# Attention inside an adaLN block: score tiles in two groups, and mask and maximum as one VectorE instruction per head and tile

## The chip, the core and the metric

The program runs on one core of one Trainium2 chip. The core has TensorE (PE: matmuls into PSUM, with the weight loads in a row of their own, PEld), VectorE (DVE), ScalarE (ACT), GpSimd (POOL) and SyncE (SP, which only issues DMAs here). The engines run in parallel, each in its own order, and wait for each other by semaphores. The metric is the device time in microseconds (us), the median of several runs.

## The reference, cut to what matters

```
h = layernorm(x) * (1 + ca) + sa                 # x: 8 batches, 512 tokens, 128 features, float32
q, k, v = split(h @ W_qkv)                       # 16 heads of 64
q, k = rotary(q), rotary(k)
s = (q @ k.T) / 8;  s = where(causal, s, -1e9)   # 512 x 512 per head
o = softmax(s) @ v
x = x + ga * (o @ W_out)
h = layernorm(x) * (1 + cb) + sb
x = x + gb * moe(h)                              # 8 experts, the best 2 per token
```

The change touches the attention alone, above all the two lines of the scores: the causal mask and the softmax.

## The kernel before, in words

Attention is done by pairs of heads: 8 batches with 8 pairs each, 64 pairs in all. A loop over slots (`all_slots`, L1419) writes the code of every engine. In a slot three pairs are in work at three stages: `q0` gets its q and k projections and the rotary turn, `q1`, one pair behind, its scores, and `q2`, two behind, the rest of its softmax, the product with v and the output product. Each engine has one function that writes its part of a slot (`pe_slot` L1125, `act_slot` L1218, `dve_slot` L1317, `pool_slot` L1371, `sp_slot` L1401). The order of lines there is the order in the engine's queue: nothing is scheduled later, and an engine that waits holds all that stands behind it.

The scores of a pair come in four tiles of 128 queries. Only the keys up to the diagonal are computed, so the tiles `TILES = (3, 0, 2, 1)` are 512, 128, 384 and 256 keys wide, each for two heads. I call them S512, S128, S384 and S256. A tile and head is a "unit" (0 to 7): units 0 and 1 are S512, 2 and 3 S128, 4 and 5 S384, 6 and 7 S256. One unit takes one PSUM bank. S512 and S384 share banks 2 and 3, S128 and S256 share banks 4 and 5, so S384 can start only when units 0 and 1 have been read by the exponential.

After the scores (`pe_scores`, on 64 rows of the PE array per head) VectorE adds the mask to the diagonal block of both heads (`dve_mask`, L1276) and takes the negated maximum over both (`dve_max`, L1283). ACT computes exp(s - max) with its row sum (`act_exp`, L1171). PE transposes the result block by block (`pe_turn_prob`, L1090) in six turns "3a", "3b", "0", "2a", "2b", "1" of 4, 4, 2, 3, 3 and 4 blocks, which alternate between the PSUM banks 6 and 7. ACT or DVE stores each turn to SBUF (`act_store` L1192, `dve_store` L1298), which frees its bank for the turn after the next. DVE inverts the row sums (L1290), ACT spreads them (`act_rep`, L1215), PE transposes them (`pe_turn_sum`, L1099) and ACT copies them to `rs` (L1209). Then come the product with v (`pe_values`, L1112), its scaling (`dve_ot`, L1306), the output product (`pe_out`, L1121) and its addition to x (`dve_acc`, L1314).

Two banks hold projections. Bank W1 holds k, is read by `dve_u` and `dve_t` (L1262, L1267), and later in the slot holds the output product until `dve_acc` has read it: `pe_qk` (L1027 to L1034) waits for `v_acc`, the `dve_acc` of the slot before. Bank W0 holds q, then the product with v, then the next tile of v (`pe_v`, L1048), which ACT copies (L1203) and whose copy the q half of `pe_qk` waits for. The route functions (`route_pe` and others) put the normalisation and expert routing of other batches into some slots.

Of the kernel before, what the change touches and what calls it, by code (L numbers as in the profile page):

```python
# [12 lines left out]
P = 128  # L13
# [32 lines left out]
MASKED = -1e30  # L46

# [40 lines left out]
def adaln_kernel(nc, x_in, w_qkv, w_out, gate_w, expert_bias, w_up, w_down, c_t, w_mod,  # L88
                 cos_in, sin_in, ident_in, tri_in, rank_in, const_in, out, xs, ys, parts, gates):
    ctx = ExitStack()  # L90
    with ctx:
# [689 lines left out]
        tri = sb(att, "tri", [P, P])  # L781
# [187 lines left out]
        with ExitStack() as ph:  # L969
# [14 lines left out]
             v_u, v_t, v_tk, v_tri, v_max, v_ev, v_rden, v_ot, g_qk, g_lo, g_wo, d_ur) = (  # L984
                sem("b_" + n) for n in (
                    "pqk", "pv", "ps", "pt", "pr", "pvp", "pout", "aexp", "aev", "ahi", "av", "ar", "arep",
                    "vu", "vt", "vtk", "vtri", "vmax", "vev", "vrden", "vot", "gqk", "glo", "gwo",
# [86 lines left out]
            def pe_turn_prob(e, q, u):  # L1074
                n, at = q.n, TURNS.index(u)
                e.wait_ge(a_exp, NU * n + READ[u][-1] + 1)
                if u == "3a":
                    if due(2 * n):
                        e.wait_ge(v_ev, 2 * n)
                elif u == "3b":  # L1080
                    if due(4 * n):
                        e.wait_ge(a_ev, 4 * n)
                elif u == "2a":
                    e.wait_ge(v_ev, 2 * n + 1)
                else:
                    e.wait_ge(a_ev, 4 * n + {"0": 1, "2b": 2, "1": 3}[u])
# [8 lines left out]
            def pe_turn_sum(e, q):  # L1095
                e.wait_ge(a_rep, q.n + 1)
                e.wait_ge(v_tk, min(q.n + 3, STEPS))
                for i in range(TB):
                    mm = e.transpose(ps[:, W1, i * P:(i + 1) * P],  # L1099
# [3 lines left out]
            def pe_values(e, q):  # L1103
# [4 lines left out]
                e.wait_ge(v_t, min(n + 3, STEPS))  # L1108
                v, first = val[q.group], (q.hp % GP) * P
# [15 lines left out]
            def pe_slot(e, i, c):  # L1125
# [7 lines left out]
                if q1.live:  # L1133
                    pe_scores(e, q1, 0)
                if q2.live:
# [3 lines left out]
                if q1.live:  # L1139
                    pe_scores(e, q1, 1)  # L1140
                if q2.live:
                    pe_values(e, q2)
                if q1.live:
                    pe_turn_prob(e, q1, "3a")
                    pe_scores(e, q1, 2)
                if q2.live:
                    pe_out(e, q2)
                if q1.live:
                    pe_turn_prob(e, q1, "3b")
                if v.live:  # L1150
                    pe_v(e, v)
                if c in SPARE:
                    if q1.live:
                        e.wait_ge(a_ev, 4 * q1.n + 1)
                    elif q2.live:
                        e.wait_ge(v_ev, 2 * q2.n + 2)
                    route_pe(e, i, c)
                if q1.live:
                    pe_scores(e, q1, 3)

            def act_exp(e, q, unit):
# [3 lines left out]
                e.wait_ge(v_max, TB * n + idx + 1)  # L1165
# [3 lines left out]
                if unit == 0 and due(n - 1):  # L1169
                    e.wait_ge(v_rden, n - 1)  # L1170
                e.activation(prob[:, unit, 0:w], ps[:, bank_s(idx) + j, 0:w], ACT.Exp,  # L1171
                             bias=nmax[:, q.par, idx, j:j + 1],
# [13 lines left out]
            def act_store(e, q, u):  # L1186
                n = q.n
                e.wait_ge(p_t, 6 * n + TURNS.index(u) + 1)
                if u == "3a" and due(n - 1):
                    e.wait_ge(p_vp, n - 1)  # L1190
# [14 lines left out]
            def act_r(e, q):  # L1205
# [3 lines left out]
                e.copy(rs[:], ps[:, W1, :]).then_inc(a_r, 1)  # L1209
# [8 lines left out]
            def act_slot(e, i, c):  # L1218
# [3 lines left out]
                if q2.live:  # L1222
                    act_exp(e, q2, 5)
                    act_exp(e, q2, 6)
                    act_exp(e, q2, 7)
                    act_store(e, q2, "0")
                    act_store(e, q2, "2a")
                    act_rep(e, q2)
# [5 lines left out]
                if q1.live:  # L1234
# [4 lines left out]
                    act_store(e, q1, "3a")  # L1239
                route_act_part(e, i, c, 1)  # L1240
                if (i, c) == (0, 2):

                    act_v(e, v)
                if q0.live:
                    act_hi(e, q0, 1)
                    act_hi(e, q0, 0)
# [5 lines left out]
                if q1.live:  # L1252
                    act_exp(e, q1, 4)
# [16 lines left out]
            def dve_mask(e, q, idx):  # L1270
                w = (TILES[idx] + 1) * P
                bank = bank_s(idx)
                at = TB * q.n + idx + 1
                e.wait_ge(p_s, at)
                block_ = ps[:, bank:bank + 2, w - P:w]
                e.tensor_tensor(block_, block_, tri[:].unsqueeze(1).to_broadcast([P, 2, P]),  # L1276
                                op=ALU.add).then_inc(v_tri, 1)

            def dve_max(e, q, idx):
                w = (TILES[idx] + 1) * P  # L1280
                bank = bank_s(idx)
                e.wait_ge(v_tri, TB * q.n + idx + 1)
                e.tensor_reduce(nmax[:, q.par, idx, :], ps[:, bank:bank + 2, 0:w], AX.X, ALU.max,  # L1283
# [763 lines left out]
```

## Time and profile before

| | |
|---|---|
| runs | 994.35, 997.01 and 1002.05 us; median 997.01 |
| profiled execution | span 996.9 us (the page gives no other time for it) |
| PE | 907.6 us busy, 91% |
| PE weight loads | 659.0 us, 66% |
| DVE | 830.6 us, 83% |
| ACT | 740.4 us, 74% |
| POOL | 570.1 us, 57% |

The attention fills the span from about 20 to 800 us. The rest is the expert part and the end, which the change leaves alone. Busy time of matmuls is from start to a modelled end, and neighbours overlap, so the starts of matmuls say more than their durations.

### The profile page before, as it was taken

The page shows a single profiled execution, that of the slowest core. Times are in us where ns is not written, and L with a number is a line of the kernel's source. Part 1 is how long each engine was busy: PE and PEld are TensorE (multiplying, and loading weights), DVE is VectorE, ACT ScalarE, POOL GpSimd, SP SyncE. Part 2 cuts the span into 40 slices and gives each one's busy share as a digit, 9 for nine tenths or more (in the row PEclk, how much of TensorE's full clock was granted, in tenths as well). Part 3 has the DMA queues.
Part 4 walks back from the last instruction along what each step waited for, and adds up shares of the span by engine and source line. Part 5 has one row for each costly group of instructions (what it writes and reads, how often), then busy time and mean ns, then how long its engine had stood idle before and what let it go on. Part 6 is the DMA issues. An engine that isn't in the chain of part 4 may idle for free. (4 is left out here: it accounts for less than half of the span.)

```text
span 996.9 us, 21240 instructions
## 1 busy us (share of the span) xinstructions
PE 907.6 (91%) x6278; PEld 659.0 (66%) x6278; DVE 830.6 (83%) x1816; ACT 740.4 (74%) x2070; POOL 570.1 (57%) x687
## 2 busy tenths in 40 slices
PE   5699999999999999999999999999999778999930
PEld 3466667676676677666766767677667556888820
DVE  6588888788988888888888888888998678899847
ACT  4487788878787887788778877787777654777725
POOL 1445456545666477657755675767466356765532
PEclk9799999999999999999999999999999989999975
DMA  8234443333344434433344434333443347899844
GB/s 250 81 93 105 111 109 95 94 93 104 94 109 113 117 99 124 115 93 94 108 118 107 110 112 118 96 100 111 110 108 96 110 162 274 290 317 321 311 136 131
DMA packets 124575, 135.53 MB, mean 136 GB/s; under 512 B 13837, under 2 KB 108571, under 8 KB 120496
## 3 DMA queue, kind: packets, MB, share of 16 engines
q1 hardware_dynamic: 118768, 122.42, 42.5%
q0 software_dynamic: 4544, 8.93, 2.7%
q10 hardware_dynamic: 1152, 2.85, 0.8%
q8 instruction: 52, 0.85, 0.3%
q14 instruction: 59, 0.48, 0.2%
HBM read 51.53 MB, written 39.49 MB: 91 GB/s over the span
## 5 line engine op out<-in xcount | busy, mean ns | idle before, releaser
L1364 POOL TENSOR_TENSOR four<-four 128x512 f32<-128x512 f32 x128 | 161.1, 1280 | 278.7 <-DVE ot L1306 178.2
L1171 ACT ACTIVATE prob<-ps,nmax 128x512 f32<-128x512 f32 (+3 forms) x512 | 264.4, 531 | 51.6 <-DVE nmax L1283 50.9
L1283 DVE TENSOR_REDUCE nmax<-ps 128x2 f32<-128x1024 f32 (+3 forms) x256 | 211.0, 824 | 8.8
L1090 PE MATMUL ps<-ident,prob 128*128 128x128 f32 x1280 | 192.4, 280 | 9.3 <-ACT probt L1192 4.9
L1090 PEld LDWEIGHTS ps<-ident,prob 128*128 128x128 f32 x1280 | 142.3, 141 | 60.3 <-ACT prob L1171 32.8
L1368 POOL TENSOR_TENSOR qk_lo<-four,qk_hi 128x512 fp32r<-128x512 f32 x128 | 163.4, 1300 | 1.5 <-ACT qk_hi L1199 1.5
L1276 DVE TENSOR_TENSOR ps<-ps,tri 128x256 f32<-128x256 f32 x256 | 109.4, 427 | 53.8 <-PE ps L1069 53.3
L1112 PE MATMUL ps<-probt,val 128*64 128x512 f32 (+3 forms) x1024 | 152.6, 440 | 0.0
L1192 ACT COPY probt<-ps 128x512 f32<-128x512 f32 (+2 forms) x256 | 125.2, 524 | 21.1 <-PE ps L1090 21.1
L1199 ACT CAST qk_hi<-four 128x512 fp32r<-128x512 f32 x128 | 79.4, 622 | 79.0 <-POOL four L1364 78.3
L1112 PEld LDWEIGHTS ps<-probt,val 128*64 128x64 f32 x1024 | 68.0, 137 | 74.0 <-issue 59.9
L1064 PE MATMUL ps<-qk_hi 64*128 64x512 f32 (+3 forms) x256 | 105.6, 412 | 5.2 <-POOL qk_lo L1368 5.2
L1990 POOL DMA_INDIRECT results<-y,to_i x78 | 82.3, 1055 | 47.4 <-DVE y L1821 28.8
L1262 DVE TENSOR_TENSOR four<-ps,turn_s 128x1024 f32<-128x1024 f32 x64 | 78.4, 1225 | 35.4 <-PE ps L1034 30.9
L1171 ACT ACTIVATION_READ_ACCUMULATOR prob<-ps,nmax 128x1 f32 x512 | 106.1, 207 | 0.0
L1065 PE MATMUL ps<-qk_hi 64*128 64x512 f32 (+3 forms) x256 | 105.6, 413 | 0.0
L1911 ACT ACTIVATE hf<-ps 128x256 f32<-128x256 f32 (+1 forms) x120 | 53.9, 449 | 39.5 <-PE ps L1762 39.0
L1064 PEld LDWEIGHTS ps<-qk_hi 64*128 64x128 f32 x256 | 47.2, 185 | 53.9 <-issue 33.6
L1067 PE MATMUL ps<-qk_hi,qk_lo 64*128 64x512 f32 (+3 forms) x256 | 82.1, 321 | 0.0
L1066 PE MATMUL ps<-qk_hi,qk_lo 64*128 64x512 f32 (+3 forms) x256 | 82.0, 320 | 0.0
L1069 PE MATMUL ps<-qk_lo,qk_hi 64*128 64x512 f32 (+3 forms) x256 | 82.0, 320 | 0.0
L1068 PE MATMUL ps<-qk_lo,qk_hi 64*128 64x512 f32 (+3 forms) x256 | 82.0, 320 | 0.0
(276 smaller groups left out, 2241.5 us busy)
## 6 DMA issues: line engine op xcount, KB each, us to landing
four<-four SPq DMA_DIRECT2D x252, 128.0 KB
wt<-parts SPq DMA_DIRECT2D x24, 1024.0 KB, 7.2
slots<-fill SPq DMA_DIRECT2D x64, 288.0 KB, 2.8
parts<-split SPq DMA_DIRECT2D x64, 128.0 KB, 2.3
wq_lo<-parts SPq DMA_DIRECT2D x6, 1024.0 KB, 6.3
hb<-h_hi SPq DMA_DIRECT2D x64, 64.0 KB, 2.3
hb<-h_lo SPq DMA_DIRECT2D x64, 64.0 KB, 2.0
plain<-results SPq DMA_DIRECT2D x8, 512.0 KB, 7.5
```

Of the source, the lines that this page charges most:

```text
L1064: e.matmul(o0, hi[top_, 0, cols], hi[top_, 1, 0:w], start=True, stop=False)
L1065: e.matmul(o1, hi[low_, 0, cols], hi[low_, 1, 0:w], start=True, stop=False)
L1067: e.matmul(o1, lo[low_, 0, cols], hi[low_, 1, 0:w], start=False, stop=False)
L1090: mm = e.transpose(ps[:, PT + at % 2, at_block * P:(at_block + 1) * P], prob[:, unit, kk * P:(kk + 1) * P], ident[:])
L1112: mm = e.matmul(ps[j * HD:(j + 1) * HD, W0, kk * P:S], v[:, kk, first + j * HD:first + (j + 1) * HD], probt[q.par][:, j, kk, kk * P:S], st ...
L1171: e.activation(prob[:, unit, 0:w], ps[:, bank_s(idx) + j, 0:w], ACT.Exp, bias=nmax[:, q.par, idx, j:j + 1], accum_out=den[:, q.par, 2 * i ...
L1192: e.copy(dst, src).then_inc(a_ev, 1)
L1276: e.tensor_tensor(block_, block_, tri[:].unsqueeze(1).to_broadcast([P, 2, P]), op=ALU.add).then_inc(v_tri, 1)
L1283: e.tensor_reduce(nmax[:, q.par, idx, :], ps[:, bank:bank + 2, 0:w], AX.X, ALU.max, negate=True).then_inc(v_max, 1)
L1364: e.tensor_tensor(qk[:, cols], tt[:, cols], ur[:, cols], op=ALU.add).then_inc(g_qk, 1)
L1368: e.tensor_tensor(qk_lo[q.par][:, half, :], qk[:, half * S:(half + 1) * S], qk_hi[q.par][:, half, :], op=ALU.subtract).then_inc(g_lo, 1)
L1990: e.indirect_dma_start(ys, bass.IndirectOffsetOnAxis(to_i[:, j % Y, t:t + 1], 0), y4[:, j % Y, t, :], None, bounds_check=2 * B * S - 1, oo ...
```

## The change

On PE the slot is written in another order. Before: projections, turns "0" and "2a", S512, turns "2b" and "1", the sum, S128, values, turn "3a", S384, output, turn "3b", v, routing, S256. Now: projections, turns "0", "2a", "2b", "1", the sum, S512, S128, values, S384, S256, turns "3a" and "3b", output, v, routing. The transposed sum goes to bank 6 in place of W1. The turns "3a" and "3b" are both stored by DVE, and "0", "2a", "2b", "1" all by ACT ("3a" was ACT's, "2b" DVE's).

On DVE the mask and the maximum of a unit are one `tensor_tensor_reduce`: it adds a mask as wide as the tile (`tri` now has 512 columns, all zero but the last 128), multiplies by -1, writes the result to the scores' bank and reduces it by minimum. ACT's exponential now takes scale -1 and waits for one unit in place of a tile of two. All eight maxima of a pair are taken in the slot of its scores; before, S256's were left to the next slot, and so were the exponentials 5 to 7 on ACT.

```diff
+HIGHEST = 3e38
...
-        tri = sb(att, "tri", [P, P])
+        tri = sb(att, "tri", [P, S])
...
                 if u == "3a":
-                    if due(2 * n):
-                        e.wait_ge(v_ev, 2 * n)
+                    if due(4 * n - 1):
+                        e.wait_ge(a_ev, 4 * n - 1)
+                    if due(n):
+                        e.wait_ge(a_r, n)
                 elif u == "3b":
                     if due(4 * n):
                         e.wait_ge(a_ev, 4 * n)
-                elif u == "2a":
-                    e.wait_ge(v_ev, 2 * n + 1)
+                elif u in ("0", "2a"):
+                    e.wait_ge(v_ev, 2 * n + {"0": 1, "2a": 2}[u])
                 else:
-                    e.wait_ge(a_ev, 4 * n + {"0": 1, "2b": 2, "1": 3}[u])
+                    e.wait_ge(a_ev, 4 * n + {"2b": 1, "1": 2}[u])
...
             def pe_turn_sum(e, q):
                 e.wait_ge(a_rep, q.n + 1)
-                e.wait_ge(v_tk, min(q.n + 3, STEPS))
+                e.wait_ge(a_ev, 4 * q.n + 3)
                 for i in range(TB):
-                    mm = e.transpose(ps[:, W1, i * P:(i + 1) * P],
+                    mm = e.transpose(ps[:, PT, i * P:(i + 1) * P],
                                      rrep[:, i, :, :].rearrange("p j f -> p (j f)"), ident[:])
...
+                e.wait_ge(v_tk, min(n + 3, STEPS))
...
@@ -1130,46 +1134,42 @@
                     spare_read(e, i, c - 1)
                     pe_turn_prob(e, q2, "0")
                     pe_turn_prob(e, q2, "2a")
-                if q1.live:
-                    pe_scores(e, q1, 0)
-                if q2.live:
                     pe_turn_prob(e, q2, "2b")
                     pe_turn_prob(e, q2, "1")
                     pe_turn_sum(e, q2)
                 if q1.live:
+                    pe_scores(e, q1, 0)
                     pe_scores(e, q1, 1)
                 if q2.live:
                     pe_values(e, q2)
                 if q1.live:
+                    pe_scores(e, q1, 2)
+                    pe_scores(e, q1, 3)
                     pe_turn_prob(e, q1, "3a")
-                    pe_scores(e, q1, 2)
+                    pe_turn_prob(e, q1, "3b")
                 if q2.live:
                     pe_out(e, q2)
-                if q1.live:
-                    pe_turn_prob(e, q1, "3b")
                 if v.live:
                     pe_v(e, v)
                 if c in SPARE:
                     if q1.live:
-                        e.wait_ge(a_ev, 4 * q1.n + 1)
+                        e.wait_ge(v_ev, 2 * q1.n + 1)
                     elif q2.live:
-                        e.wait_ge(v_ev, 2 * q2.n + 2)
+                        e.wait_ge(a_r, q2.n + 1)
                     route_pe(e, i, c)
-                if q1.live:
-                    pe_scores(e, q1, 3)
...
-                e.wait_ge(v_max, TB * n + idx + 1)
+                e.wait_ge(v_max, NU * n + unit + 1)
...
-                             bias=nmax[:, q.par, idx, j:j + 1],
+                             bias=nmax[:, q.par, idx, j:j + 1], scale=-1.0,
...
-                if u == "3a" and due(n - 1):
-                    e.wait_ge(p_vp, n - 1)
...
-                e.copy(rs[:], ps[:, W1, :]).then_inc(a_r, 1)
+                e.copy(rs[:], ps[:, PT, :]).then_inc(a_r, 1)
...
                 if q2.live:
-                    act_exp(e, q2, 5)
-                    act_exp(e, q2, 6)
-                    act_exp(e, q2, 7)
+                    act_rep(e, q2)
                     act_store(e, q2, "0")
                     act_store(e, q2, "2a")
-                    act_rep(e, q2)
+                    act_store(e, q2, "2b")
                     act_store(e, q2, "1")
                     act_r(e, q2)
                 route_act_part(e, i, c, 0)
...
-                    act_store(e, q1, "3a")
                 route_act_part(e, i, c, 1)
                 if (i, c) == (0, 2):
 
                     act_v(e, v)
+                if q1.live:
+                    act_exp(e, q1, 4)
+                    act_exp(e, q1, 5)
                 if q0.live:
                     act_hi(e, q0, 1)
+                if q1.live:
+                    act_exp(e, q1, 6)
+                    act_exp(e, q1, 7)
+                if q0.live:
                     act_hi(e, q0, 0)
                 if v.live and (i, c) != (0, 2):
                     act_v(e, v)
                 if (i, c) == (0, 1):
 
                     group_root(e, 1, s_var, s_root)
-                if q1.live:
-                    act_exp(e, q1, 4)
...
-            def dve_mask(e, q, idx):
+            def dve_peak(e, q, unit):
+                idx, j = unit // 2, unit % 2
                 w = (TILES[idx] + 1) * P
-                bank = bank_s(idx)
-                at = TB * q.n + idx + 1
-                e.wait_ge(p_s, at)
-                block_ = ps[:, bank:bank + 2, w - P:w]
-                e.tensor_tensor(block_, block_, tri[:].unsqueeze(1).to_broadcast([P, 2, P]),
-                                op=ALU.add).then_inc(v_tri, 1)
-
-            def dve_max(e, q, idx):
-                w = (TILES[idx] + 1) * P
-                bank = bank_s(idx)
-                e.wait_ge(v_tri, TB * q.n + idx + 1)
-                e.tensor_reduce(nmax[:, q.par, idx, :], ps[:, bank:bank + 2, 0:w], AX.X, ALU.max,
-                                negate=True).then_inc(v_max, 1)
+                e.wait_ge(p_s, TB * q.n + idx + 1)
+                block_ = ps[:, bank_s(idx) + j, 0:w]
+                e.tensor_tensor_reduce(block_, block_, tri[:, S - w:S], -1.0, HIGHEST, ALU.add, ALU.min,
+                                       nmax[:, q.par, idx, j:j + 1]).then_inc(v_max, 1)
...
-                if u == "3b" and due(n - 1):
+                if u == "3a" and due(n - 1):
...
             def dve_slot(e, i, c):
                 q0, q1, q2 = pairs(i, c)
                 if q2.live:
-                    dve_mask(e, q2, 3)
-                    dve_max(e, q2, 3)
+                    dve_rden(e, q2)
                 if q0.live:
                     dve_u(e, q0)
-                if q2.live:
-                    dve_rden(e, q2)
-                if q0.live:
...
-                if q2.live:
-                    dve_store(e, q2, "2b")
                 if q1.live:
-                    dve_mask(e, q1, 0)
-                    dve_max(e, q1, 0)
-                    dve_mask(e, q1, 1)
-                    dve_max(e, q1, 1)
+                    for unit in range(4):
+                        dve_peak(e, q1, unit)
                 route_dve(e, i, c)
...
                 if q2.live:
                     dve_ot(e, q2)
                 if q1.live:
-                    dve_mask(e, q1, 2)
-                    dve_max(e, q1, 2)
+                    for unit in range(4, NU):
+                        dve_peak(e, q1, unit)
+                    dve_store(e, q1, "3a")
+                    dve_store(e, q1, "3b")
                 if q2.live:
                     dve_acc(e, q2)
-                if q1.live:
-                    dve_store(e, q1, "3b")
                 route_dve_last(e, i, c)
...
-        "tri": np.triu(np.full((P, P), MASKED, np.float32), 1),
+        "tri": np.concatenate([np.zeros((P, S - P), np.float32), np.triu(np.full((P, P), MASKED, np.float32), 1)], 1),
```

PE's queue from the end of the projections (L1034) to the start of S128, first before and then with the change (L1090 and, one for one, L1093 are turns, L1099 and L1102 the sum, L1064 to L1070 scores):

```order
L1034 MATMUL ps<-h_lo,wq_hi 128x512
L1090 MATMUL ps<-ident,prob 128x128 x5
L1064 MATMUL ps<-qk_hi 128x512
L1065 MATMUL ps<-qk_hi 128x512
L1066 MATMUL ps<-qk_hi,qk_lo 128x512
L1067 MATMUL ps<-qk_hi,qk_lo 128x512
L1068 MATMUL ps<-qk_lo,qk_hi 128x512
L1069 MATMUL ps<-qk_lo,qk_hi 128x512
L1090 MATMUL ps<-ident,prob 128x128 x7
L1099 MATMUL ps<-ident,rrep 128x128 x4
L1064 MATMUL ps<-qk_hi 128x128
```

```order
L1035 MATMUL ps<-h_lo,wq_hi 128x512
L1093 MATMUL ps<-ident,prob 128x128 x12
L1102 MATMUL ps<-ident,rrep 128x128 x4
L1065 MATMUL ps<-qk_hi 128x512
L1066 MATMUL ps<-qk_hi 128x512
L1067 MATMUL ps<-qk_hi,qk_lo 128x512
L1068 MATMUL ps<-qk_hi,qk_lo 128x512
L1069 MATMUL ps<-qk_lo,qk_hi 128x512
L1070 MATMUL ps<-qk_lo,qk_hi 128x512
L1065 MATMUL ps<-qk_hi 128x128
```

The turns "2b" and "1" moved ahead of S512, so that twelve turn blocks and the sum's four now stand in one piece, and S128 follows S512 directly.

VectorE's queue from the scaling of the values' product (`ot`) on, in a slot without routing work, with the semaphores that each instruction waits for, first before, then with the change (ISA is the new instruction; each one is followed by one that writes the 128x1 result `nmax`):

```order
L1306 TENSOR_TENSOR ot<-ps,rs 128x512 [waits b_pout,b_ar,b_pvp]
L1276 TENSOR_TENSOR ps<-ps,tri 128x2x128 [waits b_ps]
L1283 TENSOR_REDUCE nmax<-ps 128x2 [waits b_vtri]
L1314 TENSOR_TENSOR x_all<-ps,x_all 128x512 [waits v_acc,b_pout]
L1298 COPY probt<-ps 128x4x128 [waits b_pvp,b_pt]
L1276 TENSOR_TENSOR ps<-ps,tri 128x2x128 [waits b_ps]
L1283 TENSOR_REDUCE nmax<-ps 128x2 [waits b_vtri]
L1262 TENSOR_TENSOR four<-ps,turn_s 128x1024 [waits b_gqk,b_pqk]
```

```order
L1298 TENSOR_TENSOR ot<-ps,rs 128x512 [waits b_pout,b_ar,b_pvp]
L1275 ISA ps,nmax<-ps,tri 128x384 [waits b_ps]
L1275 ISA nmax 128x1
L1275 ISA ps,nmax<-ps,tri 128x384 [waits b_ps]
L1275 ISA nmax 128x1
L1275 ISA ps,nmax<-ps,tri 128x256 [waits b_ps]
L1275 ISA nmax 128x1
L1275 ISA ps,nmax<-ps,tri 128x256 [waits b_ps]
L1275 ISA nmax 128x1
L1290 COPY probt<-ps 128x4x128 [waits b_pvp,b_pt]
L1290 COPY probt<-ps 128x4x128 [waits b_pt]
L1306 TENSOR_TENSOR x_all<-ps,x_all 128x512 [waits v_acc,b_pout]
```

The addition to x, whose reader is PE's next projection, stood behind one mask and one maximum. It now stands behind four pairs of the new instructions and two stores.

## Rows read from the trace of the kernel before

**Rows 1.** Groups by line and shape, 100 to 700 us: line, form, count | busy, mean ns.
```profile
L1262 DVE TENSOR_TENSOR four<-ps,turn_s 128x1024 f32<-128x1024 f32 x51 | 62.5, 1225 | 25.3 <-PE ps L1034 25.3
L1192 ACT COPY probt<-ps 128x384 f32<-128x384 f32 x51 | 26.6, 521 | 0.0
L1192 ACT COPY probt<-ps 128x256 f32<-128x256 f32 x51 | 20.0, 392 | 0.0
```

**Rows 2.** Timeline of PE, one slot without routing: start, duration, engine, line.
```profile
118.34 0.71 PE L1090 MATMUL ps<-ident,prob 128*128 128x128 f32 x5
118.97 0.50 PE L1064 MATMUL ps<-qk_hi 64*128 64x512 f32 x1
...
119.87 0.98 PE L1090 MATMUL ps<-ident,prob 128*128 128x128 f32 x7
120.69 0.60 PE L1099 MATMUL ps<-ident,rrep 128*128 128x128 f32 x4
121.22 0.32 PE L1064 MATMUL ps<-qk_hi 64*128 64x128 f32 x1
...
121.70 2.38 PE L1112 MATMUL ps<-probt,val 128*64 128x512 f32 x16
124.00 0.66 PE L1090 MATMUL ps<-ident,prob 128*128 128x128 f32 x4
124.62 0.44 PE L1064 MATMUL ps<-qk_hi 64*128 64x384 f32 x1
...
125.34 1.16 PE L1121 MATMUL ps<-wog,ot 128*128 128x128 f32 x8
126.34 0.60 PE L1090 MATMUL ps<-ident,prob 128*128 128x128 f32 x4
126.69 0.48 PE L1048 MATMUL ps<-wq_hi,hb 128*128 128x512 f32 x1
...
127.57 0.38 PE L1064 MATMUL ps<-qk_hi 64*128 64x256 f32 x1
...
128.12 0.50 PE L1027 MATMUL ps<-h_hi,wq_hi 128*128 128x512 f32 x1
...
129.62 0.60 PE L1090 MATMUL ps<-ident,prob 128*128 128x128 f32 x4
```

**Rows 3.** Timeline of DVE in the same slot, with idle time before.
```profile
119.68 0.19 DVE L1290 RECIPROCAL rden<-den 128x8 f32<-128x8 f32 x1
119.79 1.24 DVE L1267 TENSOR_TENSOR four<-ps,turn_c 128x512 f32<-128x512 f32 x2
...
124.12 0.69 DVE L1306 TENSOR_TENSOR ot<-ps,rs 128x512 f32<-128x512 f32 x1 [0.24 <-PE ps L1112]
125.46 0.43 DVE L1276 TENSOR_TENSOR ps<-ps,tri 128x256 f32<-128x256 f32 x1 [0.64 <-PE ps L1069]
...
126.80 0.68 DVE L1314 TENSOR_TENSOR x_all<-ps,x_all 128x512 f32<-128x512 f32 x1
127.39 0.68 DVE L1298 COPY probt<-ps 128x512 f32<-128x512 f32 x1
```

**Rows 4.** Timeline of ACT in the same slot.
```profile
120.89 0.59 ACT L1192 COPY probt<-ps 128x512 f32<-128x512 f32 x1 [0.37 <-PE ps L1090]
...
123.12 0.69 ACT L1171 ACTIVATE prob<-ps,nmax 128x512 f32<-128x512 f32 x1 [0.96 <-DVE nmax L1283]
...
123.80 0.68 ACT L1171 ACTIVATE prob<-ps,nmax 128x512 f32<-128x512 f32 x1
```

**Rows 5.** Timeline of all engines, 249 to 250 us.
```profile
249.17 0.78 ACT L1192 COPY probt<-ps 128x256 f32<-128x256 f32 x2
...
249.71 0.52 PE L1090 MATMUL ps<-ident,prob 128*128 128x128 f32 x3 [0.15 <-ACT probt L1192]
```

**Rows 6.** Windows of 6 us: PE, PEld, DVE, ACT, POOL busy, then PEclk.
```profile
778.00:784.00 6.00, 5.31 (x42) 3.19 (x40) 3.61 (x10) 4.89 (x17) 4.33 (x5) 1.00 0.13 40
...
790.00:796.00 6.00, 4.27 (x19) 2.76 (x21) 1.66 (x8) 4.56 (x10) 0.00 (x0) 0.72 0.68 221
```

More of the change, by code:

```diff
@@ L983, in adaln_kernel @@
             (p_qk, p_v, p_s, p_t, p_r, p_vp, p_out, a_exp, a_ev, a_hi, a_v, a_r, a_rep,
-             v_u, v_t, v_tk, v_tri, v_max, v_ev, v_rden, v_ot, g_qk, g_lo, g_wo, d_ur) = (
+             v_u, v_t, v_tk, v_max, v_ev, v_rden, v_ot, g_qk, g_lo, g_wo, d_ur) = (
                 sem("b_" + n) for n in (
                     "pqk", "pv", "ps", "pt", "pr", "pvp", "pout", "aexp", "aev", "ahi", "av", "ar", "arep",
-                    "vu", "vt", "vtk", "vtri", "vmax", "vev", "vrden", "vot", "gqk", "glo", "gwo",
+                    "vu", "vt", "vtk", "vmax", "vev", "vrden", "vot", "gqk", "glo", "gwo",
                     "dur"))
```

## The prediction, made before the changed kernel ran

> **What bounds the kernel now.** I read the groups by line and shape first, for the length of a slot. The rotary multiply `uu` runs once per slot and 51 times in the 600 us from 100 to 700 [rows 1], so a slot takes 600 / 51 = 11.76 us. I then listed the starts on TensorE through one slot without routing work [rows 2], from 118.34 to 129.62: 11.28 us. Start to start, the pieces are: turns "0" and "2a" 0.63, S512 0.90, turns "2b" and "1" 0.82, sum 0.53, S128 0.48, values 2.30, turn "3a" 0.62, S384 0.72, output 1.00, turn "3b" 0.35, v 0.88, S256 0.55, projections 1.50. None of these pieces carries a wait, so PE's stream is the bound, and the other 0.48 us of an average slot are routing matmuls and short waits. Third, the timelines of VectorE and ScalarE in the same slot [rows 3, 4], not for what they cost (they hide now) but for how soon each is done after PE. That is what the new order depends on.
>
> **The gain on PE.** A turn of four blocks takes 0.35 where full-array work stands on both sides, and 0.62 where it stands between the values and S384, which use part of the array [rows 2]. The 0.27 between them is one leaving and one entering of the partial mode, so 0.27 per change of mode, about 0.13 of it on each side. Before, a slot has nine such changes. Now it has four: sum to S512, S128 to values, values to S384, S256 to turns. Five fewer are worth 5 x 0.27 = 1.35 us, if nothing else holds PE.
>
> **What now holds PE, first place: the projections.** Let 0 be the start of S384, right after the values. PE's own order brings it to the next projections after S384 0.59, S256 0.42, turns 0.48 and 0.35, output 0.87 and v 0.75 (the pieces above, less 0.13 for each mode change gone, plus 0.13 for the new one): 3.46, or about 4.0 with routing. But the k half of the projections writes the bank that the addition to x reads, and in VectorE's queue this addition now stands last:
> - `ot` starts 0.12 after the values' successor starts (124.12 against 124.00) and frees the engine at 0.71.
> - The first maximum of S384 can start at 0.84 (125.46 against 124.62) [rows 2, 3].
> - A VectorE instruction costs 1.045 ns per column: 1225 ns for 1024 [rows 1] and 690 for 512 [rows 3]. Two of 512 columns start 0.59 apart (126.80, 127.39), so the fixed part is 0.59 - 0.535 = 0.055 us. The new instruction and its 128x1 result write are in no row. For the first I take a plain two-input instruction of that width. For the second the nearest row is the reciprocal of 8 columns, behind which the next starts after 0.11 [rows 3], so 0.10. The two bounds are below.
> - The four maxima (2 x 384 + 2 x 256 = 1280 columns) take 1.34 + 4 x 0.155 = 1.96, to 2.80. The stores "3a" and "3b" take 0.59 each, to 3.98. The addition ends 0.68 later, at 4.66.
> - PE starts 0.15 after the end of what it waits for: the first of the two stores at 249.17 takes 0.39 and PE restarts at 249.71 [rows 1, 5]. Projections at 4.81.
>
> So PE waits 1.35 us there without routing and about 0.8 with it. In front of the addition stood one mask and one maximum and no store. Routing matmuls, which cost time before, are free now.
>
> **Second place: the turns.** The projections take 1.50, to 6.31. The twelve blocks of "0", "2a", "2b", "1" and the sum's four used to have S512 in their midst, which hid ACT's stores. Now bank 6 goes "0", "2b", sum and bank 7 goes "2a", "1", each after ACT's store of the one before. A block takes 0.82 / 7 = 0.117, and its result can be read 0.20 after the last block's slot: ACT's store of turn "1" starts at 120.89, 1.02 after the seven blocks start [rows 2, 4]. Then:
> - "0" is ready at 6.31 + 0.23 + 0.20 = 6.74, stored (0.39) at 7.13; "2b" starts at 7.28.
> - "2a" is ready at 7.09, and stored (0.52) from 7.10 to 7.62; "1" starts at 7.77.
> - "2b" is ready at 7.28 + 0.35 + 0.20 = 7.83, stored at 8.35; the sum starts at 8.50, and S512 0.53 later, at 9.03.
>
> These are 2.72 us for work that took 0.63 + 0.82 + 0.53 = 1.98: a loss of 0.74.
>
> **The ring closes** with S512 and S128 (0.90 + 0.48 - 0.27 = 1.11) and the values, 2.30: the next S384 could start at 12.44. It also needs the exponentials of units 0 and 1. S512 can be read 1.02 after its start (S384's 0.84, and 0.18 because it takes 0.90 in place of 0.72), at 10.05. The first maximum takes 0.535 + 0.155 = 0.69, the second is out 0.79 after its start, at 11.53, the second exponential 0.68 [rows 4] and its sum 0.10 later, and PE 0.15 after that: 12.46. Both say 12.45.
>
> **The sum.** A slot grows by 12.45 - 11.76 = 0.69 us. There are 64 pairs, and about 61 slots have all three stages. 61 x 0.69 = 42 us on the span of 996.9, which is also the median of the runs (997.01). Forecast: **1039 us**. Edits at nothing: the swap of stores (ACT gives 0.59 and takes 0.52, DVE the other way round) is in the chains above; the wider `tri` is loaded once, beside other loads at the start; no DMA moves on SP, and POOL's adds still wait for `ot`. The VectorE time that the fusion saves lies in idle time, since PE waits for the last instruction in the queue and not for a free engine.
>
> **Bounds of the unknown.** Low: the result write costs nothing, which takes 4 x 0.10 from the first chain. The ring is 12.04, + 0.28 x 61 = 17 us: 1014. High: the result write starts only when the main instruction has ended (0.155 beyond its columns in place of 0.055) and holds the queue for a small instruction's whole 0.19. Each maximum costs 0.345 beyond its columns, 0.19 more. The first chain grows by 0.76, and the exponential's by a further 0.28, to 13.50: + 1.74 x 61 = 106, 1103 us. I take the value near the low end because VectorE's rows overlap: 0.59 from start to start for instructions of 0.68.
>
> **Rivals.**
> - *PE stays the bound (faster).* If the addition and the stores come in time, a slot is 11.76 - 1.35 = 10.41 and the time is 997 - 82 = 915. For it: PE's rows are full now, and 1.35 is a large saving. Against it: the addition would have to end by 3.3, and it stands behind 1.96 + 1.18 of other VectorE work that begins at 0.84. Half of the gain would be 956. Chance 0.14 for anything more than 1% faster.
> - *The chains are a little shorter than summed (no change).* The ring must come to 11.9 or less: a free result write and 0.04 less at each of four waits. Within 1%: 0.11.
> - *VectorE drains behind each instruction*: the high bound, 1103. Against it is the 0.59 spacing; for it, that the result write depends on the instruction ahead of it. Chance 0.10. The Trainium skill, "VectorE: DVE Perf Modes", section "The DRAIN you can't avoid", speaks for this one and against the change: the next operation does not start until the pipeline has emptied, and the page prices a float32 operation at (columns + 151) / 0.96 ns. Estimated from that page, a maximum with its write has 0.315 us beyond its columns and the time would be about 1092. By that rule two 512-wide instructions would start 0.69 apart; the trace has 0.59 and disagrees.
> - *The granted clock falls.* PE would work about 10.4 of 12.45 us. At 5.31 of 6 us busy the granted clock was 1.00, at 4.27 of 6 it was 0.72, after a stretch of waits [rows 6]; the new share lies between. At 0.72 in all of the attention PE's part is 14.4 us and the time about 1160. Chance 0.05.
> - That the change doesn't do what it says is excluded by the two queues shown.
>
> **Numbers.** The forecast's own case (1014 to 1065) has 0.58, and 0.02 is left for other delays. About 1% can be told from no change here. Slower by over 1%: 0.58 + 0.10 + 0.05 + 0.02 = 0.75. Within 1%: 0.11. Faster: 0.14. The range of 992 to 1090 holds the forecast's case, most of "no change" and most of the drained case; outside are the faster case, the clock and the far end of the drained one.
>
> **What would show it.** Right: slots of nearly one length, about 12.4 us, with and without routing; on PE a wait of about 1 us before the first projection, released by the addition to x, and two or three waits of 0.15 to 0.3 in the turns, released by ACT's stores; four scores' starts without a gap; VectorE less busy in total yet with the addition ending about 4.7 after S384's start. Wrong: projections that follow v directly; turns without waits; a result write that starts after its main instruction's end (then the high bound); a granted clock under 1.00 inside the attention.

## The result, and the profile after

The changed kernel takes **1023.23 us** (median of 4 runs, 1022.75 to 1023.82) against 999.53 for the kernel before on the same chip: ratio 1.022, 95% interval 1.019 to 1.026. Forecast were 1039 us and 992 to 1090. The growth of the median is 24 us; the forecast had 42. The profiled execution has a span of 1021.0 us, before 996.9. One execution of an experiment's kernel below (S512 between, addition in the middle) took 1912 us, for no reason on record, and stands in no ratio.

First the page: busy time and share of each engine.

```profile
PE 886.0 (87%) x6278; PEld 661.2 (65%) x6278; DVE 771.2 (76%) x2328; ACT 749.1 (73%) x2070; POOL 572.6 (56%) x687
```

PE and VectorE both do less than before (907.6 and 830.6 us), and the kernel is slower: the signature of a wait, not of an engine. So the next view is the waits from 100 to 700 us (engine, line waited at <- engine and line waited for: total us, times, longest).

```profile
PEld ps L1028 <- DVE x_all L1306: 33.5, 39, 1.2
PE ps L1028 <- DVE x_all L1306: 23.9, 42, 0.9
PE ps L1093 <- ACT probt L1190: 11.1, 49, 0.2
```

The first projection (L1028) waits for the addition to x (L1306), the turns (L1093) for ACT's stores (L1190): the two places of the forecast. Groups of the same stretch (busy time, mean ns of one, idle time before them), to be read against [rows 1]:

```profile
L1262 DVE TENSOR_TENSOR four<-ps,turn_s 128x1024 f32<-128x1024 f32 x49 | 60.0, 1225 | 77.3 <-PE ps L1035 77.3
L1275 DVE DVE_READ_ACCUMULATOR2_ANT nmax<- 128x1 f32 x393 | 56.1, 143 | 0.0
L1275 DVE CUSTOM_DVE_ANT_0 ps<-ps,tri 128x384 f32<-128x384 f32 x98 | 53.0, 582 | 1.0
L1275 DVE CUSTOM_DVE_ANT_0 ps<-ps,tri 128x256 f32<-128x256 f32 x98 | 41.6, 467 | 0.0
```

From start to start of the rotary multiply a slot now takes 12.16 to 12.26 us in 46 of 48 cases, with routing and without, mean 12.20; before it ranged from 11.28 to 12.81, mean 11.79. The difference, 0.41, times 61 slots is 25 us of the 24 measured. The new instruction appears as two: the main one (582 ns for 384 columns) and a 128x1 read-out of 143 ns.

PE's timeline (start, duration), a slot with a routing piece (L357), to be read against [rows 2]:

```profile
399.92 0.40 PE L1051 MATMUL ps<-wq_hi,hb 128*128 128x512 f32 x1
400.15 0.95 PE L357 MATMUL ps<-gate_sb,ht 128*128 128x8 f32 x8
401.08 0.51 PE L1028 MATMUL ps<-h_hi,wq_hi 128*128 128x512 f32 x1
...
402.58 0.71 PE L1093 MATMUL ps<-ident,prob 128*128 128x128 f32 x5
403.52 1.06 PE L1093 MATMUL ps<-ident,prob 128*128 128x128 f32 x7 [0.23 <-ACT probt L1190]
404.70 0.63 PE L1102 MATMUL ps<-ident,rrep 128*128 128x128 f32 x4
405.25 0.49 PE L1065 MATMUL ps<-qk_hi 64*128 64x512 f32 x1
...
406.06 0.22 PE L1065 MATMUL ps<-qk_hi 64*128 64x128 f32 x1
...
406.43 2.38 PE L1116 MATMUL ps<-probt,val 128*64 128x512 f32 x16
408.74 0.44 PE L1065 MATMUL ps<-qk_hi 64*128 64x384 f32 x1
...
409.37 0.28 PE L1065 MATMUL ps<-qk_hi 64*128 64x256 f32 x1
...
409.81 1.09 PE L1093 MATMUL ps<-ident,prob 128*128 128x128 f32 x8
410.74 1.06 PE L1125 MATMUL ps<-wog,ot 128*128 128x128 f32 x8
411.55 0.48 PE L1049 MATMUL ps<-wq_hi,hb 128*128 128x512 f32 x1
```

VectorE's timeline, first the addition that lets 401.08 start, then the queue behind the next S384, against [rows 3]:

```profile
400.34 0.68 DVE L1306 TENSOR_TENSOR x_all<-ps,x_all 128x512 f32<-128x512 f32 x1
...
408.85 0.69 DVE L1298 TENSOR_TENSOR ot<-ps,rs 128x512 f32<-128x512 f32 x1 [0.42 <-PE ps L1116]
409.57 0.57 DVE L1275 CUSTOM_DVE_ANT_0 ps<-ps,tri 128x384 f32<-128x384 f32 x1
410.05 0.14 DVE L1275 DVE_READ_ACCUMULATOR2_ANT nmax<- 128x1 f32 x1
410.05 0.60 DVE L1275 CUSTOM_DVE_ANT_0 ps<-ps,tri 128x384 f32<-128x384 f32 x1
410.57 0.14 DVE L1275 DVE_READ_ACCUMULATOR2_ANT nmax<- 128x1 f32 x1
410.57 0.47 DVE L1275 CUSTOM_DVE_ANT_0 ps<-ps,tri 128x256 f32<-128x256 f32 x1
...
411.33 1.28 DVE L1290 COPY probt<-ps 128x512 f32<-128x512 f32 x2
412.53 0.68 DVE L1306 TENSOR_TENSOR x_all<-ps,x_all 128x512 f32<-128x512 f32 x1
```

Count from S384 at 408.74: first maximum 0.83, maxima over 2.59, stores over 3.79, addition over 4.47. A projection starts 0.06 after the addition's end (400.34 + 0.68 = 401.02, and 401.08), so 4.53. Then, in the PE rows, projections 1.50, turns and sum 2.67 (402.58 to 405.25), S512 with S128 1.18, values 2.31: together 12.19, the slot. PE's own work from S384 to the projections is 3.59 without routing, so it waits 0.94 there.

### The profile page after: what moved, and what is told of

Its sections match the earlier page's. It is cut to its first block and busy times, and to the rows that moved or that the text cites. A ratio compares the mean times of both kernels' runs of the same rounds, so it can differ in the third digit from the quotient of the medians.

```text
span 1021.0 us, 21688 instructions
## 1 busy us (share of the span) xinstructions
PE 886.0 (87%) x6278; PEld 661.2 (65%) x6278; DVE 771.2 (76%) x2328; ACT 749.1 (73%) x2070; POOL 572.6 (56%) x687
## 5 line engine op out<-in xcount | busy, mean ns | idle before, releaser
L1275 DVE CUSTOM_DVE_ANT_0 ps<-ps,tri 128x512 f32<-128x512 f32 (+3 forms) x512 | 236.3, 524 | 74.0 <-PE ps L1070 72.8
L1093 PE MATMUL ps<-ident,prob 128*128 128x128 f32 x1280 | 185.1, 280 | 17.1 <-ACT probt L1190 15.4
L1093 PEld LDWEIGHTS ps<-ident,prob 128*128 128x128 f32 x1280 | 141.5, 142 | 56.0 <-issue 29.0
L1190 ACT COPY probt<-ps 128x384 f32<-128x384 f32 (+2 forms) x256 | 120.0, 480 | 58.4 <-PE ps L1093 52.8
L1171 ACT ACTIVATION_READ_ACCUMULATOR prob<-ps,nmax 128x1 f32 x512 | 103.7, 202 | 0.0
L1065 PE MATMUL ps<-qk_hi 64*128 64x512 f32 (+3 forms) x256 | 92.3, 360 | 5.6 <-POOL qk_lo L1352 3.8
L1066 PE MATMUL ps<-qk_hi 64*128 64x512 f32 (+3 forms) x256 | 92.0, 359 | 0.0
L1290 DVE COPY probt<-ps 128x512 f32<-128x512 f32 x128 | 82.3, 685 | 0.0
L1070 PE MATMUL ps<-qk_lo,qk_hi 64*128 64x512 f32 (+3 forms) x256 | 82.2, 321 | 0.0
L1267 DVE TENSOR_TENSOR four<-ps,turn_c 128x512 f32<-128x512 f32 x128 | 81.8, 681 | 0.0
```

The lines of the kernel that those rows point to most:

```text
L1065: e.matmul(o0, hi[top_, 0, cols], hi[top_, 1, 0:w], start=True, stop=False)
L1066: e.matmul(o1, hi[low_, 0, cols], hi[low_, 1, 0:w], start=True, stop=False)
L1093: mm = e.transpose(ps[:, PT + at % 2, at_block * P:(at_block + 1) * P], prob[:, unit, kk * P:(kk + 1) * P], ident[:])
L1190: e.copy(dst, src).then_inc(a_ev, 1)
L1275: e.tensor_tensor_reduce(block_, block_, tri[:, S - w:S], -1.0, HIGHEST, ALU.add, ALU.min, nmax[:, q.par, idx, j:j + 1]).then_inc(v_max, 1)
L1290: e.tensor_copy(dst, src).then_inc(v_ev, 1)
```

## The experiments

On the chips of these runs the kernel before took 1031 to 1037 us, more than in the first runs; the part behind the attention is the longer one there (258 us from the last rotary multiply on in the run with the fusion alone, 230 before), the slots of the attention hardly (11.86 against 11.79). So each kernel is compared by its ratio to the kernel before on its own chip, and by its slots. "Order" is the change's order of work, "fused" the one-instruction mask and maximum.

**Fused alone**, in the order of the kernel before (PE, DVE and ACT lists as there, `dve_peak` in place of `dve_mask` and `dve_max`).

> The kernel before with mask and maximum as one instruction per head and tile, and its order of work unchanged. Theory (PE's stream bounds the old order and VectorE's saving lies in idle time): a slot of 11.7 to 11.8 us and no difference to before, 990 to 1002 us, with VectorE about 60 us less busy. Rival (the new instruction with its result write is itself what makes the changed kernel slow): 1010 us or more.

Ratio 0.996, 0.994 to 0.998; slots 11.25 to 12.84, mean 11.86. By the forecast's bound of 1% that is no difference.

**Order alone**, with mask and maximum apart again:

```diff
-                    for unit in range(4, NU):
-                        dve_peak(e, q1, unit)
+                    dve_mask(e, q1, 2)
+                    dve_max(e, q1, 2)
+                    dve_mask(e, q1, 3)
+                    dve_max(e, q1, 3)
```

> The changed kernel's order with mask and maximum apart, as before. Theory (two rings close over VectorE's maxima): the two masks and maxima of S384 and S256 take 2.39 us in place of 1.76 (+0.63) ahead of the addition, and S384 has to wait for exponentials that start 0.9 us later behind S512 (+0.83), so a slot is 13.5 to 13.7 us, about 1105 to 1115 us. Rival (only the order of PE counts, the maxima are covered): about 1021 to 1030 us.

Ratio 1.117, 1.113 to 1.121; every slot 13.71. Its waits:

```profile
PEld ps L1065 <- ACT prob L1171: 49.3, 86, 0.9
PEld ps L1028 <- DVE x_all L1314: 42.2, 40, 1.7
```

So the loss belongs to the order. The fusion is worth 0.4% where VectorE is covered and 9.5% of the time before (1.117 to 1.022) where the order has put it on the path. PE's starts (means from 100 to 700 us) tell where the 1.51 us more than in the changed kernel's slot are: S384 starts 3.06 after the values in place of 2.30, since it waits 0.68 for the exponentials of units 0 and 1; from v to the projections 0.46 more pass, mostly the wait for the addition; S384 and S256 take 0.17 more and the projections 0.12. The first two are the rings of the expectation, which had 0.83 and 0.63 for them.

**The addition to x ahead of both stores:**

```diff
+                    dve_acc(e, q2)
                     dve_store(e, q1, "3a")
                     dve_store(e, q1, "3b")
-                    dve_acc(e, q2)
```

> The changed kernel with one move in VectorE's queue: the addition to x stands ahead of the stores of turns 3a and 3b. In the changed kernel a slot is 12.18 us and the first projection starts 4.5 us after S384, released by the addition. Theory A (the addition is all that holds the projections): the output product is readable about 3.0 after S384's start, the addition ends at 3.7, PE's own order is ready at 3.6, so the projections start at 3.75 and a slot is 11.4 us, about 975 us in all. Theory B (ScalarE's copy of v is next in line, only 0.2 us behind): the copy still ends at 5.15, the q half of the projections waits for it, the turns start at 6.05 as now (6.02), and a slot stays at 12.15 to 12.2 us, about 1021 us, with the wait on the k half replaced by one of about 0.7 us on the q half, released by ACT's copy.

Ratio 1.036, 1.031 to 1.041: slots without routing 12.16, as before the edit, with routing 12.5 to 13.0. The timeline of PE, of two slots, shows why the 0.7 us gained at the first projection are gone at once.

```profile
405.68 1.06 PE L357 MATMUL ps<-gate_sb,ht 128*128 128x8 f32 x8 [0.68 <-DVE probt L1290]
...
418.07 0.50 PE L1028 MATMUL ps<-h_hi,wq_hi 128*128 128x512 f32 x1
...
419.44 0.50 PE L1033 MATMUL ps<-h_hi,wq_hi 128*128 128x512 f32 x1 [0.41 <-ACT val L1201]
```

The q half (L1033) waits for ACT's copy of v (L1201), which stands behind four exponentials. Routing (L357) works in bank 6 and waits for store "3a", now behind the addition: a wait that was not forecast.

**The same, with the copy of v between the exponentials of units 6 and 7:**

```diff
                 if q1.live:
                     act_exp(e, q1, 6)
+                if v.live and (i, c) != (0, 2):
+                    act_v(e, v)
+                if q1.live:
                     act_exp(e, q1, 7)
                 if q0.live:
                     act_hi(e, q0, 0)
-                if v.live and (i, c) != (0, 2):
-                    act_v(e, v)
```

> As e1, and in ScalarE's queue the copy of v stands between the exponentials of units 6 and 7 in place of behind unit 7 and the last rounding of q. Theory A and theory B both expect the projections at about 3.75 after S384 without a wait on the q half, so that the turns start at 5.25 in place of 6.02: a slot of 11.4 to 11.6 us without routing and about 11.7 with, 980 to 990 us in all, still with the turns' waits of about 0.7 us. If it stays above 1010 us, a third chain (the spread of the inverse sums, or the stores of 3a and 3b) holds the turns.

Ratio 1.018, 1.015 to 1.022. Slots without routing fall to 11.49, as forecast, which shows the copy of v as the second chain, 0.03 us behind the first. Slots with routing stay at 12.1 to 13.0, the mean of all is 12.18, and the total misses its forecast.

**The addition between store "3a" and store "3b", v early:**

> As e2, but VectorE's queue ends with store 3a, the addition to x, store 3b. Routing on PE waits for store 3a, which in e1 and e2 came behind the addition and made slots with routing 12.1 to 13.0 us long while those without were 11.49 in e2. Expected: store 3a ends at 3.3 after S384's start, the addition at 3.9, projections at 3.95: slots without routing 11.65 to 11.7 us (0.15 to 0.2 longer than e2's), slots with routing 11.7 to 12.2. About 20 to 25 us less than the changed kernel, a ratio of 0.99 to 1.01 to the kernel before. If routing slots stay at 12.5, something other than store 3a holds routing.

Ratio 1.001, 0.998 to 1.004. Slots 11.6 without routing, 11.9 to 12.3 with it, one in eight 12.77; mean 11.87. The whole loss of the change is gone with two instructions moved, and no part of the kernel before's time is won.

**Turns "0" and "2a" ahead of the projections** (against the changed kernel):

```diff
-                if q0.live:
-                    pe_qk(e, q0)
                 if q2.live:
                     spare_read(e, i, c - 1)
                     pe_turn_prob(e, q2, "0")
                     pe_turn_prob(e, q2, "2a")
+                if q0.live:
+                    pe_qk(e, q0)
```

> The changed kernel with turns 0 and 2a ahead of the projections on PE (and ACT's stores of them ahead of its spread of the inverse sums). Theory (the turns lose 0.7 us because nothing covers ACT's stores, and PE idles in front of the projections anyway): the two turns fall into that idle time, the projections still start at 4.5 and cover the stores, and from the end of the projections to S512 1.7 us pass in place of 2.67. A slot of 11.2 to 11.3 us without routing and up to 11.8 with, against 12.18: about 40 us less than the changed kernel, a ratio of about 0.98 to the kernel before. Rival (what holds S512 is the spread of the sums or another chain of ACT, not the turns' banks): a slot of 11.9 or more.

Slots without routing took 11.22, as forecast (11.2 to 11.3): there the turns fill the wait for the addition, and the stores run under the projections. But the ratio is 1.028, 1.024 to 1.033, since slots with routing rise to 12 to 15.5:

```profile
PEld ps L1093 <- ACT ht L334: 12.6, 6, 2.5
PEld ps L1093 <- ACT rows L345: 12.3, 5, 2.8
```

Turn "0" now follows routing directly and waits until ACT has read routing's results out of bank 6, up to 2.8 us.

**S512 back between the turns "2a" and "2b":**

```diff
                     pe_turn_prob(e, q2, "2a")
+                if q1.live:
+                    pe_scores(e, q1, 0)
+                if q2.live:
                     pe_turn_prob(e, q2, "2b")
                     pe_turn_prob(e, q2, "1")
                     pe_turn_sum(e, q2)
                 if q1.live:
-                    pe_scores(e, q1, 0)
                     pe_scores(e, q1, 1)
```

> The changed kernel with S512 back between turn 2a and turn 2b, as in the kernel before: two more changes of array mode (0.54 by my sum) and a cover for ACT's stores of 0 and 2a (0.7 us of waits less). The addition still starts the projections at 4.5. Theory: from the projections' end to the values 0.63 + 0.90 + 0.82 + 0.53 + 0.48 = 3.36 us in place of 3.85, a slot of 11.7 us, a ratio of about 1.00 to the kernel before. Rival (the waits in the turns are covered by something else later): 12.1 to 12.2 us as now.

Ratio 1.019, 1.014 to 1.024; most slots 12.11, where 11.7 was forecast, and the mean 12.21, that of the changed kernel (12.20). From the projections' end to the values the pieces are 0.64, 0.89 (S512), 1.21 (turns "2b" and "1"), 0.56 and 0.48: 3.78 against 3.85. The sum, now in bank 6 behind turn "2b", waits for its store; in the kernel before it went to W1. So S512 hides one store and uncovers the other.

**Both of the last ideas that had helped slots (S512 between; addition in the middle, v early):**

> e7 and e5 together: both places mended. If the two places are separate terms of one ring, their gains add: projections at 3.95 and 3.36 us from their end to the values, a slot of 11.1 to 11.2 us without routing and 11.2 to 11.7 with, a ratio of 0.96 to 0.98 to the kernel before. If another chain takes over (exponentials before S384, POOL's rounding before S512), it stays above 11.4.

Ratio 1.030, 1.025 to 1.036, slots 11.8 to 12.7, mean 12.36: worse than either. A fourth chain has taken over, GpSimd's low part of q and k:

```profile
PEld ps L1065 <- POOL qk_lo L1356: 29.7, 48, 1.0
```

**Turn "0" ahead only in slots whose bank 6 no routing has just used, with the addition in the middle and v early:**

> The changed kernel with the addition to x between stores 3a and 3b and ScalarE's copy of v early (as in the run where no-routing slots fell to 11.6), and turn 0 ahead of the projections in those slots alone whose bank 6 no routing has just used (3 of 8); ScalarE does store 0 before its copy for the next unit there. Theory (each chain that holds the slot can be shortened separately; turns without cover cost 0.12 a block): four blocks then run while the addition is still going on, 0.46 us, so those slots take 11.1 to 11.2, the others stay at 11.6 to 12.3; mean near 11.70, time 0.985 to 0.995 of the kernel before. Rival (another chain stands right behind, as in the last runs): store 3b, now after the addition, ends after the turn is wanted, and those slots stay at 11.5 to 11.6; ratio 1.00.

Ratio 0.996, 0.993 to 0.998. The slots with the turn ahead took 11.14 to 11.3 in most rounds, as forecast; the others rose from 11.59 to 11.74, from 12.3 to 12.46 and from 12.77 to 12.91. Those 0.15 stand in the turns, and the likely cause is the edit's other half, ACT's store of "0" ahead of its copy for the sum in every slot; this was not tried apart. Mean 11.83, forecast 11.70.

**The order of before, fused, with S384 ahead of turn "3a":**

```diff
+                    pe_scores(e, q1, 2)
                     pe_turn_prob(e, q1, "3a")
-                    pe_scores(e, q1, 2)
```

> The order of the kernel before with the one-instruction mask and maximum, and S384 moved ahead of turn 3a, straight behind S512 and S128's neighbours of its own kind, so that TensorE changes between score tiles and other work once less. Theory: a change costs TensorE 0.15 us, and TensorE binds the slot there: 11.86 - 0.15 = 11.7 in the mean, ratio 0.996 - 0.010 = 0.986. Rival (the turns slide under the next wait, or an exponential is late): slots stay at 11.86, ratio 0.996.

**Ratio 0.987, 0.982 to 0.991**, mean slot 11.68: both as forecast (0.986, 11.7). It beats both kernels. In PE's timeline the pieces from the values to the output product are, in the order S384, "3a":

```profile
352.68 2.38 PE L1113 MATMUL ps<-probt,val 128*64 128x512 f32 x16
354.98 0.44 PE L1065 MATMUL ps<-qk_hi 64*128 64x384 f32 x1
...
355.71 0.66 PE L1091 MATMUL ps<-ident,prob 128*128 128x128 f32 x4
356.20 1.06 PE L1122 MATMUL ps<-wog,ot 128*128 128x128 f32 x8
357.10 0.60 PE L1091 MATMUL ps<-ident,prob 128*128 128x128 f32 x4
```

These are 3.52 us to the output product; in [rows 2] the same work took 3.64 (121.70 to 125.34). The output product is shorter too, 0.90 in place of 1.00. Up to turn "3b" it is 4.42 against 4.64: one change of mode fewer is 0.22 here, not the 0.15 of the theory. Not all of it reaches the slot. The shortest slots, without routing, fall only from 11.25 to 11.18, as S512 and the turns and sum behind it take about 0.1 longer; the mean falls by 0.18 from that of the fusion alone, by 0.20 without routing (11.52 to 11.32, counted from values to values) and by 0.16 with it (12.13 to 11.97). That the total came out at 0.987 is therefore in part luck: the saving was larger than priced, and some of it was lost again.

**The same with S256 there too,** two more changes fewer:

> As the last, with S384 and S256 both right behind the values' product and ahead of turn 3a: up to three changes of kind fewer, the addition to x still before the maxima on VectorE, so that TensorE need not wait for it at the projections. Theory (TensorE binds, 0.15 a change): 11.86 - 0.45 = 11.4 in the mean, ratio about 0.96. Rival: the addition stands before the maxima, the maxima before stores, and the stores of unit 6 and 7 then come late for the turns and give 0.3 to 0.6 back: mean 11.7 to 12.0, ratio 0.985 to 1.01.

Ratio 0.991, 0.988 to 0.994, mean slot 11.78: the rival's 11.7 to 12.0. The two changes are worth 0.28 (S384 0.63 in place of 0.72, S256 0.45 of 0.55, v 0.78 of 0.87), and the projections take 0.31 more in slots without routing: the wait is at a place that neither theory named. S256 used to stand between v and the projections and hid ACT's copy of v:

```profile
PEld ps L1033 <- ACT val L1203: 26.3, 42, 1.7
```

**S384 first, and S128 directly behind S512:**

> The last order that came out ahead (that of the kernel before with the one-instruction mask and maximum and S384 ahead of turn 3a) with S128 also moved directly behind S512. One change of kind fewer again, and TensorE has 0.4 us more of work between the turns 2a and 2b. Theory (TensorE binds, 0.15 a change): mean slot 11.68 - 0.15 = 11.53, ratio 0.978. Rival (the exponentials of units 0 and 1 already end at S384's start or up to 0.25 us after it, and their maxima stand on VectorE behind store 2b, which now comes 0.3 us later): S384 waits for them and gives the 0.15 or more back, mean 11.68 to 11.9, ratio 0.987 to 1.0. I give the rival the larger chance in slots with routing.

Ratio 0.994, 0.991 to 0.997, mean 11.87. S128 used to stand between the sum and the values and hid ACT's store of turn "1":

```profile
356.31 0.60 PE L1100 MATMUL ps<-ident,rrep 128*128 128x128 f32 x4
357.14 2.37 PE L1113 MATMUL ps<-probt,val 128*64 128x512 f32 x16 [0.24 <-ACT probt L1192]
```

From the sum to the values 0.84 pass in place of 0.55; S512 and S128 save 0.26 and the turns 0.02, so the shortest slots stay at 11.18. PE's waits from 100 to 700 us show what makes the mean longer:

```profile
PE ps L1113 <- ACT probt L1192: 14.4, 44, 1.2
PE ps L1065 <- ACT prob L1171: 10.6, 21, 1.7
```

All 21 of the second are S384's first matmul, waiting for the exponentials: the rival's waiter (2.6 us in 11 slots without this move). The rival had the size right and named one of two waits.

## Why the prediction was right, point by point

- **PE's own gain.** Without its waits the slot after is S384 0.63, S256 0.44, turns 0.93, output 0.81, v 0.78, projections 1.50, twelve blocks 1.40, sum 0.53, S512 0.80, S128 0.38, values 2.30: 10.50 us against 11.28. The gain is 0.78, or 0.15 to 0.16 for each of five changes, where 0.27 was taken. The step that is wrong is the price from one short turn "3b" of 0.35: a block is 0.117, so four are 0.47, and the 0.62 of "3a" holds 0.15 of mode change. The 0.35 is less than four blocks take, and the output ahead of it takes 0.90 even without S384 beside it, against 0.81 ahead of v: the two must be priced together. The 0.15 is a mean over five, not a constant: the single change above was worth 0.22. From S384 to the projections PE was off the path, so the forecast of the slot hardly depends on it; but the rival "PE stays the bound" was overstated: a slot of 11.0 us and a gain of 0.78 x 61 = 48 us would have been its price, not 82.
- **First place, the addition to x.** Shown: the wait stands in the rows, and moving the addition takes 0.7 us off the slot as soon as the copy of v goes with it. Sizes: four maxima forecast to end at 2.80, measured 2.59; addition's end 4.66, measured 4.47; PE's restart 0.15, measured 0.06; PE's wait there 1.35, measured 0.94. The read-out is the mis-sized term. I priced it at 0.10 on top of 0.055; it starts together with the next main instruction, and a 384-column maximum costs 0.52 where another follows at once, a 256-column one 0.38. Beyond 1.045 ns per column that is 0.11 to 0.12, not 0.155.
- **Second place, the turns.** Forecast 2.72, measured 2.67. Less twelve blocks and the sum (1.40 + 0.53) the stall is 0.74, as forecast. That covering the turns is worth it was shown by the slots of 11.22 with "0" and "2a" ahead.
- **The exponentials as an equal chain** (12.46 against 12.44): they end 0.24 before S384 starts (408.50 by ACT's rows), and where S384 does wait for them, in the order alone (0.68), it starts 0.05 after that end. So this chain was near, 0.19 behind, and not equal.
- **The sum.** 12.44 forecast for this ring, 12.19 measured: -0.19 at the addition (maxima -0.21, the rest +0.02), -0.09 for PE's restart, -0.05 for the turns, +0.08 for S512, S128 and the values, where the mode changes were priced too high. 0.25 us in 61 slots are 15 of the 16 us by which 1039 is above 1023. As a growth of the slot it is 0.41 where 0.69 was forecast: two fifths of the 0.69 were terms priced too high, most of them on the same side (and a slot before of 11.76 where the starts give 11.79), and the range was wide enough for them.
- **VectorE drains.** Refuted: 410.05 and 410.57 are 0.52 apart with a main instruction of 0.60 and a read-out between. The Trainium skill, "VectorE: DVE Perf Modes", section "The DRAIN you can't avoid", has the next operation wait until the pipeline has emptied, and adds, which the prediction left out, that one that is not held starts earlier. These rows agree with the addition, not with the rule.
- **The clock.** The granted clock was 1.00 from 100 to 700 us, the higher of the two levels, with PE busy for 558.5 of the 600 and no wait at the projections longer than 0.9. The rival had no part.
- **Not foreseen:** how close the other chains stand. Copy of v 0.03 us behind the addition, store "3a" before routing, bank 6 before turn "0", the store of "2b" before the sum, GpSimd's low part. None of them moved the forecast, all of them moved the experiments.

Open: why one change of mode is worth 0.22 in one place and 0.14 to 0.16 in others, and why S384 and S256 take 0.17 longer in the order alone. The copy of v was never moved by itself.

## What to carry to other kernels

Every piece of work on the bounding engine also hides somebody's latency. Before moving it, name what it hid: here S512 hid the turns' stores, S256 the copy of v, S128 the last store, and three of the four moves that brought equal work together lost 0.3 to 0.7 us of cover for 0.28 us of mode changes saved (0.78 in the change as a whole); only S384 ahead of "3a" uncovered little. An instruction whose reader is the next slot's first should not stand last in its queue. And fusing instructions on an engine that is not the bound gives nothing (0.4%), while it may be all that makes a tighter order bearable.

## What the runs showed of the hardware that was not expected

- The fused mask and maximum runs as a main instruction (716, 582, 467 and 333 ns for 512, 384, 256 and 128 columns) and a read-out of 143 ns that overlaps its successor.
- A PE matmul starts 0.06 us after the end of the VectorE instruction it waits for (44 of 49 first projections), against 0.15 after ACT's store [rows 5] (all 49 waits in the turns).
- A change between score tiles and full-array work costs PE 0.14 us (two with S256 moved), 0.16 (five together) or 0.22 (one, S384 ahead of "3a").
